# A conditioned ternary feed-forward block on one core: mixing matmuls halved, weight scaling moved from GpSimd to ScalarE, early tiles of x loaded sooner

## What is computed

```python
masked_w = weight * mask[None, :, :]                 # (8, 512, 512)
w_bot = jnp.einsum('bg,got->bot', y, masked_w)       # (2, 512, 512)
h = jnp.einsum('bnt,bot->bno', x, w_bot) + bias
# bitlinear: _act_quant(x) @ _weight_quant(w).T
#   weight: scale = 1 / mean(|w|); clip(round(w * scale), -1, 1) / scale      (ternary)
#   act:    scale = 127 / max|row|; round(x * scale) / scale
gate = silu(bitlinear(h, w_gate)); up = bitlinear(h, w_up)    # 512 -> 2048
out = x + bitlinear(gate * up, w_down)                        # 2048 -> 512
```

## Time and profile before

| | |
|---|---|
| median of 3 runs | 487.4 us |
| the profiled execution | 488.77 us, of which span of the instructions 486.9 us |
| PE busy | 465.2 us (96% of the span) |
| DVE, ACT, POOL busy | 357.5, 215.4, 31.2 us |
| granted TensorE clock, mean | 0.993 of full speed |
| DMA | 68.62 MB, mean 141 GB/s |

### The profile page before, as it was taken

The page is one execution under the profiler, slowest core; times in us unless marked ns, Lnnn a source line. Parts: engine busy times, 40 slices in busy tenths (PEclk is TensorE's granted clock), DMA queues, the critical chain, the costliest instruction groups (busy, mean ns, idle before and its releaser), DMA issues.

```text
span 486.9 us, 6317 instructions
## 1 busy us (share of the span) xinstructions
PE 465.2 (96%) x1888; PEld 203.7 (42%) x1920; DVE 357.5 (73%) x691; ACT 215.4 (44%) x282; POOL 31.2 (6%) x21
## 2 busy tenths in 40 slices
PE   4999899999959999999999999999999999999996
PEld 1233344444324444444444444444444444444442
DVE  0211599979966887887877787878887877878883
ACT  1006643683563544445444454443454444454341
POOL 0000444207000000000000000000000000000000
PEclk9999999999988999999999999999999999999999
DMA  8999947964140336333543334443334443335444
GB/s 257 409 409 419 351 118 185 380 149 106 38 68 17 75 66 131 87 87 96 115 117 103 86 86 104 112 125 91 86 86 111 109 126 86 86 92 115 116 110 130
DMA packets 103728, 68.62 MB, mean 141 GB/s; under 512 B 87200, under 2 KB 87200, under 8 KB 102176
## 3 DMA queue, kind: packets, MB, share of 16 engines
q1 hardware_dynamic: 103712, 68.44, 51.1%
HBM read 39.06 MB, written 8.39 MB: 97 GB/s over the span
## 4 chain that ended last, share of the span: by engine, by line
PE 61%; DVE 14%; DMA 11%; issue 6%; ACT 4%; SPq 3%; POOL 0%; DVEq 0%; ACTq 0%
PE ps L465 40%; PE ps L475 20%; DMA wc<-w_gate 4%; DMA qT<-q_sb 4%; DVE h_max L333 3%; DVE h_sb L331 3%; DMA wc<-wcond 2%; DVE wc L370 2%; DVE tern_gate L322 1%; DVE tern_down L322 1%; ACT h_sb L238 1%; ACT q_sb L243 1%; ACT wc L254 1%; DVE wc L392 1%; DVE p_part L372 1%
## 5 line engine op out<-in xcount | busy, mean ns | idle before, releaser
L254 ACT ACTIVATE wc<-ps,gate_unit 128x512 f32<-128x512 f32 x128 | 87.3, 683 | 144.3 <-PE ps L465 144.3
L465 PE MATMUL ps<-tern_gate,qT 128*128 128x512 bf16 x484 | 128.7, 382 | 8.6 <-DVE wc L370 4.3
L465 PE MATMUL ps<-tern_up,qT 128*128 128x512 bf16 x510 | 132.8, 383 | 0.1
L475 PE MATMUL ps<-tern_down,wc 128*128 128x512 bf16 x510 | 129.5, 379 | 1.4 <-DMA wc<-wc 1.3
L370 DVE TENSOR_TENSOR wc<-ps,wc 128x512 f32<-128x512 f32 x128 | 88.0, 687 | 51.6 <-PE ps L465 31.8
L434 PE MATMUL ps<-w_bot,xT_sb 128*128 128x512 f32 x256 | 112.9, 596 | 1.4 <-DMA xT_sb<-xT 1.4
L372 DVE TENSOR_REDUCE p_part<-wc 128x1 f32<-128x512 f32 x128 | 87.8, 686 | 4.4
L465 PEld LDWEIGHTS ps<-tern_gate,qT 128*128 (+1 forms) x512 | 49.9, 98 | 72.1 <-issue 14.2
L261 ACT ACTIVATE wc<-wc 128x1024 bf16<-128x1024 f32 x64 | 64.2, 1051 | 34.3 <-DVE wc L392 34.3
L465 PEld LDWEIGHTS ps<-tern_up,qT 128*128 (+1 forms) x512 | 50.5, 99 | 61.7 <-issue 2.2
L475 PEld LDWEIGHTS ps<-tern_down,wc 128*128 128x128 bf16 x512 | 50.0, 98 | 62.0 <-DVE result L360 1.7
(11 more groups left out here) (37 smaller groups left out, 104.8 us busy)
## 6 DMA issues: line engine op xcount, KB each, us to landing
wc<-wcond SPq DMA_DIRECT2D x16, 512.0 KB, 12.4
xT_sb<-xT SPq DMA_DIRECT2D x32, 256.0 KB, 8.1
x_res<-x SPq DMA_DIRECT2D x32, 256.0 KB, 2.7
out<-result SPq DMA_DIRECT2D x32, 256.0 KB, 2.0
wc<-w_gate SPq DMA_DIRECT2D x4, 1024.0 KB, 17.3
wc<-w_up SPq DMA_DIRECT2D x4, 1024.0 KB, 13.4
wc<-w_down SPq DMA_DIRECT2D x4, 1024.0 KB, 8.0
tern_down<-mask SPq DMA_DIRECT2D x4, 256.0 KB, 12.7
```

The source lines that it names most:

```text
L254: nc.scalar.activation(silu[:, c % 2], ps[:, GATE + c % 2], ACT.Silu, scale=unit).then_inc(silu_ready, 1)
L465: ins = nc.tensor.matmul(ps[:, bank + c % 2], tile, w[:, c, k], start=(k == 0), stop=(k == KH - 1))
L475: ins = nc.tensor.matmul(ps[:, DOWN + par], q2T[:, par, k], tern_down[:, k], start=(k == 0), stop=(k == KI - 1))
```

## The change

There are five parts.

1. A mixing matmul has y of batch 0 in 16 columns and y of batch 1 in the other 16, so one matmul makes 16 rows of either batch. A slice takes 8 matmuls in place of 16. The blocks of `half` 0 go to bank 6 and those of `half` 1 to bank 7, with the batches' positions swapped, so that the rows of a batch lie in both banks, half of them in each.
2. The two halves have to be put together. ScalarE copies bank 6 into `w_bot` of each batch with a factor per partition that is 1 or 0 (`half_on`), 8 copies in all, and VectorE adds bank 7 with the opposite factor (`merge_halves`, 8 instructions). Batch 1 comes out with its partitions swapped in groups of 16, which the host makes up for by swapping x and the mask of batch 1.
3. The mask of batch 1 is a second array of 1 MB, loaded behind `w_up`, and applied by VectorE in 4 instructions after tile 6. That of batch 0 is applied within `merge_halves`, 4 instructions.
4. ScalarE scales the weight pieces (`scale_piece`), one per tile after `cond_round` of tiles 0 to 3, 9 to 12 and 19 to 22. The sums of `w_up` move to tiles 4 to 7, those of `w_down` to tiles 13 to 16. VectorE clips after tiles 1 to 4, 10 to 13 and 20 to 23. GpSimd keeps the sums over the partitions.
5. SP loads x tiles 6 and 7 ahead of the bias and `w_gate`, tiles 8 to 10 ahead of `w_up`, and tiles 11 and 12 ahead of its third piece.

```diff
@@ sync
+            def load_mask(b, k):
+                sp.dma_start(mask_sb[:, b, k], mask[b, :, k]).then_inc(s_mask[b][k], 16)
...
+            for t in range(EARLY, XSLOTS):
+                load_xT(t)
             sp.dma_start(bias_sb[:, :], bias.partition_broadcast(P)).then_inc(s_bias, 16)
...
-            for t in range(EARLY, XSLOTS):
-                load_xT(t)
             for a in range(PIECES):
                 if a % 2 == 0:
                     sp.wait_ge(mix_psum, 2 * (a // 2 + 3))
+                if a == 0:
+                    for t in range(XSLOTS, XSLOTS + 3):
+                        load_xT(t)
+                if a == 2:
+                    for t in range(XSLOTS + 3, AHEAD):
+                        load_xT(t)
                 load_raw(1, w_up, a)
-            for t in range(XSLOTS, AHEAD):
-                load_xT(t)
+            for k in range(KH):
+                load_mask(1, k)
@@ gpsimd
-                pool.wait_ge(mean_step, 3 * (m + 1))
-                for a in range(PIECES):
-                    nc.gpsimd.tensor_scalar(raws[m][:, a], raws[m][:, a], w_inv[:, m:m + 1], ROUND, ALU.mult, ALU.add
-                                            ).then_inc(scaled, 1)
@@ scalar
+            def scale_piece(m, a):
+                act.wait_ge(mean_step, 3 * (m + 1))
+                nc.scalar.activation(raws[m][:, a], raws[m][:, a], ACT.Copy, bias=ROUND, scale=w_inv[:, m:m + 1]
+                                     ).then_inc(scaled, 1)
...
+            for k in range(KH):
+                act.wait_ge(mix_psum, 2 * k + 1)
+                for b in range(BATCH):
+                    nc.scalar.activation(w_bot[:, b, k], ps[:, MIX], ACT.Copy, scale=half_on[:, b:b + 1]
+                                         ).then_inc(half_copied, 1)
             for a in range(PIECES):
                 abs_sum_piece(0, a)
-            abs_sum_piece(1, 0)
-            abs_sum_piece(1, 1)
...
             for t in range(LATE):
                 cond_round(t)
+                if t < PIECES:
+                    scale_piece(0, t)
+                elif t < 2 * PIECES:
+                    abs_sum_piece(1, t - PIECES)
...
@@ vector
+            def merge_halves(k):
                 for b in range(BATCH):
+                    dve.wait_ge(mix_psum, 2 * k + 2)
+                    dve.wait_ge(half_copied, 2 * k + b + 1)
+                    nc.vector.scalar_tensor_tensor(out=w_bot[:, b, k], in0=ps[:, MIX + 1], scalar=half_on[:, 1 - b:2 - b],
+                                                   in1=w_bot[:, b, k], op0=ALU.mult, op1=ALU.add).then_inc(half_merged, 1)
+                    if b == 0:
+                        apply_mask(0, k, w_bot0_ready)
...
+            piece_after = {m_t + a: (m, a) for m, m_t in enumerate((1, 10, 20)) for a in range(PIECES)}
             for t in range(LATE):
                 cond_tile(t)
+                if t == 6:
+                    for k in range(KH):
+                        apply_mask(1, k, w_bot1_ready)
                 if t in piece_after:
                     ternary_piece(*piece_after[t])
-                if t == 6:
+                if t == 9:
                     weight_mean(1)
                 if t == HALF - 1:
                     units(0)
-                if t == HALF - 1:
+                if t == 18:
                     weight_mean(2)
@@ tensor
-            def mix_products(k, b):
+            def mix_products(k):
                 if k > 0:
-                    pe.wait_ge((w_bot0_ready, w_bot1_ready)[b], k)
+                    pe.wait_ge(half_copied, 2 * k)
+                    pe.wait_ge(half_merged, 2 * k)
...
+            mix_products(0)
+            early_products(0, range(FIRST))
+            for k in range(1, KH):
+                mix_products(k)
+                early_products(k - 1, range(FIRST, EARLY))
                 early_products(k, range(FIRST))
...
+                elif t == HALF:
+                    pe.wait_ge(h_ready, t - COND_BANKS + 1)
+                    pe.wait_ge(w_bot1_ready, KH)
```

More of the change, by code:

```diff
@@ L91, in build @@
         s_bias = sem("s_bias")
-        s_mask = [sem(f"s_mask{k}") for k in range(KH)]
+        s_mask = [[sem(f"s_mask{b}_{k}") for k in range(KH)] for b in range(BATCH)]
         s_wc = [[sem(f"s_wc{k}_{i}") for i in range(4)] for k in range(KH)]
@@ L101, in build @@
         ident_ready = sem("ident_ready")
-        mix_zero = sem("mix_zero")
         fold_ready = sem("fold_ready")
         mix_w_ready = sem("mix_w_ready")
+        half_ready = sem("half_ready")
         mix_psum = sem("mix_psum")
+        half_copied = sem("half_copied")
+        half_merged = sem("half_merged")
         w_bot0_ready = sem("w_bot0_ready")
@@ L146, in load_wc @@
                     sp.dma_start(wc[:, k, 2 * i:2 * i + 2], wcond[k, :, 2 * i:2 * i + 2]).then_inc(s_wc[k][i], 16)
-                sp.dma_start(mask_sb[:, k], mask[:, k]).then_inc(s_mask[k], 16)
+                load_mask(0, k)
             def load_raw(m, src, a):
@@ L296, in mix_weights, with apply_mask @@
                                         ).then_inc(fold_ready, 1)
+                nc.vector.tensor_reduce(half_on[:, :], ident[:, :].rearrange("p (c h m) -> p h c m", h=2, m=T16), AX.XY,
+                                        ALU.add).then_inc(half_ready, 1)
                 dve.wait_ge(s_small, 16)
[L298 removed]
                 dve.wait_ge(fold_ready, 1)
[L300 to L308 removed]
+                for i, b in enumerate((0, 1, 0)):
+                    nc.vector.tensor_scalar(mix_w[:, T16 * i:T16 * i + T16], fold[:, :], y_sb[:, b:b + 1], None, ALU.mult
+                                            ).then_inc(mix_w_ready, 1)
+                dve.wait_ge(half_ready, 1)
+            def merge_halves(k):
+                for b in range(BATCH):
+                    dve.wait_ge(mix_psum, 2 * k + 2)
[4 more added lines that the diff above has]
+                        apply_mask(0, k, w_bot0_ready)
+            def apply_mask(b, k, done):
+                dve.wait_ge(half_merged, 2 * k + b + 1)
+                dve.wait_ge(s_mask[b][k], 16)
+                nc.vector.tensor_tensor(w_bot[:, b, k], w_bot[:, b, k], mask_sb[:, b, k], ALU.mult).then_inc(done, 1)
             def weight_mean(m):
@@ L437, in cond_products @@
                         ins.then_inc(cond_psum, 1)
-            def mix_products(k, b):
+            def mix_products(k):
                 if k > 0:
-                    pe.wait_ge((w_bot0_ready, w_bot1_ready)[b], k)
+                    pe.wait_ge(half_copied, 2 * k)
+                    pe.wait_ge(half_merged, 2 * k)
                 for half in range(2):
                     for c in range(4):
-                        if b == 0 and half == 0:
+                        if half == 0:
                             pe.wait_ge(s_wc[k][c], 16)
-                        ins = nc.tensor.matmul(ps[32 * c:32 * c + 32, MIX + b],
-                                               mix_w[:, b, T16 - T16 * half:T16 - T16 * half + 32],
-                                               wc[:, k, 2 * c + half], start=(half == 0), stop=(half == 1))
-                ins.then_inc(mix_psum, 1)
+                        ins = nc.tensor.matmul(ps[32 * c:32 * c + 32, MIX + half], mix_w[:, T16 * half:T16 * half + 32],
+                                               wc[:, k, 2 * c + half], start=True, stop=True)
+                    ins.then_inc(mix_psum, 1)
             def early_products(k, tiles):
@@ L477, in down @@
                     ins.then_inc(down_psum, 1)
-            pe.wait_ge(mix_w_ready, BATCH)
-            for k in range(2):
-                mix_products(k, 0)
-                mix_products(k, 1)
-                early_products(k, range(FIRST))
-            for k in range(2):
-                early_products(k, range(FIRST, EARLY))
-            for k in range(2, KH):
-                mix_products(k, 0)
-                mix_products(k, 1)
-                early_products(k, range(EARLY))
+            pe.wait_ge(mix_w_ready, 3)
+            mix_products(0)
[3 more added lines that the diff above has]
+                early_products(k - 1, range(FIRST, EARLY))
+                early_products(k, range(FIRST))
+            early_products(KH - 1, range(FIRST, EARLY))
             for t in range(EARLY, LATE):
@@ L545 @@
     tiles = x.reshape(TILES, P, HID)
+    swap = np.arange(P) ^ T16
+    xT = tiles.reshape(TILES, P, KH, P).transpose(0, 3, 2, 1)
+    xT = np.concatenate([xT[:HALF], xT[HALF:][:, swap]])
+    mask = np.asarray(L0_cond_mask).reshape(HID, KH, P).transpose(2, 1, 0)
     arrays = {
-        "xT": a(tiles.reshape(TILES, P, KH, P).transpose(0, 3, 2, 1)),
+        "xT": a(xT),
         "x": a(tiles),
@@ L551 @@
         "wcond": a(np.asarray(L0_cond_weight).reshape(G, HID, KH, BLOCKS, T16).transpose(2, 0, 4, 3, 1).reshape(KH, P, BLOCKS, HID)),
-        "mask": a(np.asarray(L0_cond_mask).reshape(HID, KH, P).transpose(2, 1, 0)),
+        "mask": a(np.stack([mask, mask[swap]])),
```

31 lines of the change are left out of this document (13 added, 18 removed).

## The result

Six runs of each kernel: 491.46 us median (490.27 to 493.23) against 487.7 (486.99 to 489.23). The ratio is 1.0076, with a 95% interval of 1.0053 to 1.0098: the changed kernel is slower, by 3.8 us between the medians. The profiled executions say 491.41 and 488.77 us, 2.64 apart, with spans of 489.5 and 486.9.

What follows compares the result with a forecast made beforehand. It took the chain of VectorE and ScalarE from 48.1 to 143.2 us as the bound. A `cond_tile` end 1.7 us later plus 1.6 for a tail wait gave 3.3, so 487.4 + 3.3 = 490.7 us, range 484.5 to 493.5.

Steps and rivals of the forecast that it cites:

- TensorE's front: First stage: halved mixing lets tile 6 start at 43.4 in place of 48.4, 6.5 us promised in TensorE's own view.
- VectorE's start: `cond_tile(0)` starts at 49.4 in place of 48.07, as two x tiles ahead of `w_gate` cost 1.3 us.
- The wait for the transpose: ScalarE before rounding tile 2: waits 6 us for tile 0's transpose behind the second mask; tile 4 starts at 69.0.
- the first rival in my list: Loose hand-overs: tile 0's transpose doesn't wait for the backlog, tiles 2 to 4 run 5 us earlier; 484; chance 0.18.
- the second: Rival that TensorE's gain arrives at the third chunk: 16 us at most, 13 with the last hand-over, 474; chance 0.04.
- TensorE's gap: At tile 12, TensorE stands from 64.3 to about 69.8 for `h_sb` of tile 4; cond products end at 131.5.
- Tiles 4 to 29: VectorE and ScalarE handing over, tile 4 to last `cond_tile`: 75.9 us in place of 73.8, ending at 144.9.
- The clips: VectorE's clips without GpSimd beside them: all near 1.2 + 0.7 us; 3 x 3.5 = 10.4 us of slow clips leave.
- The wait of the tail: ScalarE's wait for a transpose in the last run of tiles without clips: taken in full, 1.6 us.
- my other bound: The alternative for ScalarE's transpose wait in the last tiles: zero in place of 1.6 us.

Runs made afterwards that it cites:

- e5: The changed kernel with four buffers `q_sb` in place of two, so a rounding waits for the transpose four tiles before; 482.25 us, 0.9881 of the kernel before.
- e7: The changed kernel with one unused GpSimd `affine_select` added at its end, behind the all-reduces; 489.72 us, 1.0045 of the kernel before.
- e11: The changed kernel with one tiny GpSimd `tensor_scalar` behind `affine_select` at the start; 490.37 us, 1.0041 of the kernel before.
- e1: The changed kernel with the second mask's four loads issued behind the transpose of tile 1; 487.26 us, 0.9974 of the kernel before.
- e9: The kernel before with parts 1 to 3 of the change alone; 486.83 us, 0.998 of the kernel before.
- e8: The changed kernel with four buffers `q_sb` and other places for loads, sums, scalings and clips; 474.4 us, 0.9716 of the kernel before.

## Why the prediction was right

The forecast was 490.7 us, slower by the queue's backlog in front of the first transpose. Step by step:

- **TensorE's front.** Slices halved as said, and one step missing: I had mixing 1 done at 21.0 from a start near 6.4, and it starts at 11.15. The slices' arrival hid most of that. Tile 6 came at 45.0 (43.4 predicted). None of this reached the end, since TensorE then stood at tile 12.
- **VectorE's start.** `cond_tile(0)` at 49.76 (49.4).
- **The wait for the transpose.** 6.36 us (6), tile 4 at 70.08 (69.0). I added 2.6 us for the mask to the old landing of 62.0, which gave 64.6, and it landed at 65.6. In e5, e7 and e11, with the same loads ahead, it lands at 65.0, 64.8 and 64.9, so the mask is worth 2.8 to 3.6 us. The two kernels aren't level at tile 4, as I had it: 70.08 against 69.35 is 0.7 us. e1 and e5 show that this wait is the cause, e1 by shortening it and e5 by taking it away, with all other waits for transposes. The transpose didn't overtake the mask, whose last load landed by 62.9. (That was the mechanism of the first rival in my list, where I wrote the second.)
- **TensorE's gap.** It stood from 65.8 to 70.9 (64.3 to 69.8), but the cond products ended at 134.6, not 131.5. My sum took 18 tiles from 69.8; the 144 records behind the gap, at 8 to a tile, are 18 tiles in 63.7 us, 3.54 each in place of 3.43, and the start was 1.1 later. The two give 3.1. The slower tiles stand right behind the gap: the granted clock is 0.56 of full speed from 70.9 to 73.0 and 0.74 from there to 76, a cost of some 1.7 us against 18 tiles at the pace of the earlier trace rows, which I had left out. It cost nothing in the end, since the next chunk waited for VectorE in any case.
- **Tiles 4 to 29.** From 70.08 to 145.6, 75.5 us (75.9). The mean of `w_up` ready at 86.2 (85.0), the transpose of tile 7 landed at 88.7 (88.6) and the wait at tile 9 1.84 us (2.5), the mean of `w_down` ready at 117.3 (116.3), the first clip of it at 122.7 (121.9). The mask passes took 2.50 us (2.9), a scaling 1.99 (1.9).
- **The clips.** 1.21 to 1.23 and 0.69 us, in place of the 3.01 and 2.35 beside GpSimd. The first pass lies beside ScalarE's roundings; of the second passes the one at 56.14 lies beside a scaling (56.03 to 58.03) and is no longer for it. The Trainium skill, "SBUF — State Buffer", section "Who interferes with whom", has ScalarE sharing no port with VectorE; the trace agrees.
- **The wait of the tail.** I took 1.6 us from the earlier trace rows in full, and it isn't there; zero, my other bound, was right. In its place VectorE's end is 0.7 us later than my sum: 145.6 against 144.9, and 2.4 us behind the 143.2 of before.

The forecast sum was +3.3 us. The profiled executions are +2.64 apart and the medians +3.76. e7 and e11, whose traces read like the changed kernel's, have ratios of 1.0045 and 1.0041, some 2 us. A difference of 1 us between medians is thus not told apart here. The chain was right, but half of the 3.3 us was the wait of the tail, which isn't there; the trace bears out 2.4. That 490.7 stands so near to 491.46 is in part luck.

What I hadn't seen is that parts 1 to 3 alone lose nothing (e9). In the kernel before, GpSimd's slow first piece holds VectorE back until the transpose has landed. The change takes this cover away and lengthens what was under it, in one step.

## What to carry to other kernels

Before work is put into the program of an engine that waits on a DMA, look at what stands ahead of it there: in-order engines hand a wait on to every consumer behind it (here 6.36 us became 6.11 and 5.11). Count the bytes queued ahead of each small latency-bound transfer, and if a load can't be moved behind it, add buffers until nobody waits for it; here 1 MB or two buffers decided the sign. A front made shorter pays only as far as the engines behind it keep up: in the changed kernel it ended in a gap at tile 12, in e8 TensorE had no gap left.
